# Four sums of the resident weights' quarters move from VectorE to GpSimd

## What is computed

```
h  = layernorm(x)                                # x: 16 x 100 x 1024
q  = h @ Wq                                      # 32 heads of 128
k, v = concat([ctx, h]) @ Wk, ... @ Wv           # ctx: 16 x 361 x 1024; 4 kv heads of 128
x  = x + (softmax(q k^T / sqrt(128)) v) @ Wo
g  = layernorm(x);  inter = g @ c1_w.T @ c2_w.T
idx = argmax of inter in each block of 64 columns (3584 / 64 = 56 rows per token)
x  = x + relu(w1[idx] . g) @ w2t[idx]
```

## Time and profile before

| | us |
|---|---|
| median of 3 runs | 3507.02 |
| the runs | 3506.54 to 3511.08 |
| profiled execution | 3502.41 |
| its span, first to last instruction | 3500.7 |
| TensorE busy (matmul) | 3352.3 (96%) |
| VectorE busy | 2283.3 (65%) |
| ScalarE busy | 1592.1 (45%) |
| GpSimd busy | 1037.2 (30%) |

### The profile page before, as it was taken

One profiled execution on the slowest core, in us unless ns is written; L12 is line 12 of the kernel. 1 busy time (PEld: TensorE's weight loads), 2 busy tenths in 40 slices (PEclk: granted clock), 3 DMA queues, 4 the chain that ended last, 5 costly groups with the idle time before them and its releaser, 6 DMA issues. The chain is left out here.

```text
span 3500.7 us, 52890 instructions
## 1 busy us (share of the span) xinstructions
PE 3352.3 (96%) x18226; PEld 2984.2 (85%) x18226; DVE 2283.3 (65%) x3857; ACT 1592.1 (45%) x3332; POOL 1037.2 (30%) x1220
## 2 busy tenths in 40 slices
PE   6999999799999899999999899999978999999998
PEld 5888888699999899999999778778868999987777
DVE  5555567676766577777777633333337999967776
ACT  4333344344433477777777522232256666621120
POOL 0000000000000377777777210000012455536544
PEclk8999999899999999999999999999999999999999
DMA  3333333355444344333443554454435887889888
GB/s 120 106 100 100 101 97 97 93 129 138 108 129 119 110 114 115 110 111 91 115 115 88 174 134 120 146 155 121 116 125 178 283 306 269 288 311 350 286 286 309
DMA packets 490422, 556.80 MB, mean 159 GB/s; under 512 B 174276, under 2 KB 370372, under 8 KB 490212
## 3 DMA queue, kind: packets, MB, share of 16 engines
q1 hardware_dynamic: 438308, 368.12, 35.4%
q0 software_dynamic: 50848, 183.92, 15.1%
q10 hardware_dynamic: 1056, 2.10, 0.2%
HBM read 440.86 MB, written 113.18 MB: 158 GB/s over the span
## 5 line engine op out<-in xcount | busy, mean ns | idle before, releaser
L2192 PE MATMUL wo_acc<-wo_w,wo_l 128*128 128x512 f32 (+1 forms) x2496 | 577.5, 393 | 20.2 <-DVE wo_l L2142 20.2
L269 PE MATMUL kv_bank<-kv_wo,kv_so 128*128 128x512 f32 x2436 | 574.9, 395 | 16.0 <-DVE kv_wo L361 11.6
L2192 PEld LDWEIGHTS wo_acc<-wo_w,wo_l 128*128 128x128 f32 (+1 forms) x2496 | 462.7, 186 | 134.8 <-DVE wo_w L2166 19.9
L269 PEld LDWEIGHTS kv_bank<-kv_wo,kv_so 128*128 128x128 f32 x2436 | 457.9, 190 | 110.7 <-issue 17.2
L657 PE MATMUL pr_bank<-pr_xo,pr_wp 128*128 128x400 f32 x2688 | 498.4, 347 | 29.0 <-ACT pr_s L724 13.4
L657 PEld LDWEIGHTS pr_bank<-pr_xo,pr_wp 128*128 128x128 f32 x2688 | 493.2, 190 | 31.7 <-DVE pr_wp L741 24.0
L1727 PE MATMUL hid_acc<-x1t,hid_w 128*128 128x304 f32 x2688 | 400.9, 305 | 10.0 <-DVE hid_w L1843 9.9
L2467 PE MATMUL w_acc<-w_w,w_l 128*128 128x512 f32 (+1 forms) x1680 | 385.8, 392 | 9.5 <-DVE w_l L2416 5.2
L1727 PEld LDWEIGHTS hid_acc<-x1t,hid_w 128*128 128x128 f32 x2688 | 382.9, 191 | 12.2 <-DVE hid_w L1843 6.5
L2467 PEld LDWEIGHTS w_acc<-w_w,w_l 128*128 128x128 f32 (+1 forms) x1680 | 307.9, 184 | 87.1 <-DVE w_l L2416 5.2
L2142 DVE TENSOR_TENSOR wo_l<-wo_l_raw,wo_l 128x512 fp32r<-128x512 f32 (+1 forms) x208 | 139.4, 672 | 345.9 <-ACT wo_l L2115 345.8
(11 more groups left out here) (210 smaller groups left out, 4992.1 us busy)
## 6 DMA issues: line engine op xcount, KB each, us to landing
wo_l_raw<-o_scratch SPq DMA_DIRECT2D x192, 256.0 KB, 2.9
pair_raw<-in_L_xattn_Wq_dram SPq DMA_DIRECT2D x64, 512.0 KB, 5.7
q_scratch<-pr_out SPq DMA_DIRECT2D x128, 200.0 KB, 2.4
o_scratch<-o_stage SPq DMA_DIRECT2D x64, 400.0 KB, 3.4
q_raw<-q_scratch SPq DMA_DIRECT2D x64, 384.0 KB, 3.1
stage<-in_ctx_dram SPq DMA_DIRECT2D x45, 512.0 KB, 4.0
h_scratch<-c_raw SPq DMA_DIRECT2D x28, 608.0 KB
wo_w_raw<-in_L_xattn_Wo_dram SPq DMA_DIRECT2D x16, 1024.0 KB, 7.3
```

What stands on the lines that cost most here:

```text
L269: last = pe.matmul(bank[:, BANK[i], :], so[:, i, a, c, :], wo[:, i, e, c, :], start=(not opened and c == 0 and (a, e) == PAIRS[0]), stop=( ...
L2192: last = pe.matmul(acc[p][:rows, :], l[j % 2][:, a, k, :rows], w[:, c, m * per + k, :], start=(m == 0 and k == 0 and (a, c) == PAIRS[0]), ...
```

## The change

GpSimd's program gets the four sums in front of its first copies, with the same waits and the same semaphore; VectorE's loop no longer calls them. Operands, order among the sums and arithmetic stay.

```diff
--- before.py
+++ after.py
@@ -219,7 +219,26 @@
 
         @block.gpsimd
         def _(pool):
+            def sum_b(n):
+                if n == 0:
+                    pool.wait_ge(b_landed[0], 16)
+                    pool.wait_ge(b_landed[1], 16)
+                    last = pool.tensor_tensor(b12, b12, b11, ALU.subtract)
+                elif n == 1:
+                    pool.wait_ge(t_made, 1)
+                    pool.wait_ge(b_low, 2)
+                    last = pool.tensor_tensor(b22, b22, b12, ALU.subtract)
+                elif n == 2:
+                    pool.wait_ge(t_made, 2)
+                    last = pool.tensor_tensor(b11, b22, b11, ALU.subtract)
+                else:
+                    pool.wait_ge(b_low, 4)
+                    last = pool.tensor_tensor(b21, b21, b22, ALU.subtract)
+                last.then_inc(t_made, 1)
+
             pool.memset(moments[:, :], 0.0).then_inc(cleared, 1)
+            for n in range(4):
+                sum_b(n)
 
             for G in range(NG):
                 if pieces(G + 1) > pieces(G):
@@ -413,29 +432,10 @@
                 dve.tensor_tensor(sf[:, 1], pair_raw[G % 2][:, 0, half:, :], sf[:, 1],
                                   ALU.subtract).then_inc(s_made, 1)
 
-            def sum_b(n):
-                if n == 0:
-                    dve.wait_ge(b_landed[0], 16)
-                    dve.wait_ge(b_landed[1], 16)
-                    last = dve.tensor_tensor(b12, b12, b11, ALU.subtract)
-                elif n == 1:
-                    dve.wait_ge(t_made, 1)
-                    dve.wait_ge(b_low, 2)
-                    last = dve.tensor_tensor(b22, b22, b12, ALU.subtract)
-                elif n == 2:
-                    dve.wait_ge(t_made, 2)
-                    last = dve.tensor_tensor(b11, b22, b11, ALU.subtract)
-                else:
-                    dve.wait_ge(b_low, 4)
-                    last = dve.tensor_tensor(b21, b21, b22, ALU.subtract)
-                last.then_inc(t_made, 1)
-
             first_sums(0)
             for k in range(7):
                 low_s(0, k)
                 low_b(k)
-                if k in (0, 1, 2, 3):
-                    sum_b(k)
                 if k == 1:
                     last_sum(0)
             for G in range(NG):
```

## The result

The changed kernel is slower by 0.3%: 3518.08 us median of 7 runs (3516.25 to 3523.79) beside 3508.43 us of the kernel before (7 runs, 3502.27 to 3513.41). The ratio is 1.0031, with a 95% interval of 1.002 to 1.0041, so 7 to 14 us. Its profiled execution took 3519.39 us.

A forecast was written before the change was run, and what follows sets the result against it. The prediction took the start to end with block 4's landing, queued behind a store that waits on VectorE's chain. Exclusion made that chain 8.5 us later; added to the 3507.02 us median this gave 3515.5 us, range 3504.0 to 3520.5.

The forecast's parts named there:

- What bounds the start: First stage: the start ends when context block 4 lands; its load is queued on SyncE behind the first store.
- The 2.92 us: First stage: from the end of VectorE's last low part (46.13) to block 4's issue (49.05), left alone by the change.
- The sum's own length: One 2048-column subtraction on GpSimd: 4.6 us, estimated from rows of 384 and 512 columns.
- Exclusion both ways: GpSimd sums and VectorE's two-SBUF-input instructions shut each other out for whole instructions; chance 0.55.
- The walk: Step-by-step schedule of the start with exclusion, from 16.5 us: last low part ends at 54.7, 8.5 us later.
- First phase: From 16.5 us: GpSimd's first sum and VectorE's low part, small part, low part in turn, 9.6 us, to 26.1.
- Carried one for one: From the start into everything behind it: the 8.5 us delay passes on in full, as no wait has slack.
- the forecast's own: Whole kernel: time range for blocking by whole instructions, 3514 to 3517 us around 3515.5.
- a sign of being wrong: Stages after the first: each keeps its old length; the forecast is wrong if they change by themselves.
- Without exclusion: Rival, start of the first stage: GpSimd doesn't hold VectorE; 2.1 us less, 3504.9, up to 3507; chance 0.15.
- Starved sums: Rival, start: GpSimd gets in only when VectorE runs dry; 13.1 us later, 3520.1; chance of its group 0.17.
- Partial blocking: Rival, start: GpSimd holds the read path for part of a sum; -2 to +7 us, 3505 to 3514; chance 0.13.

The follow-up runs named there:

- kernel with early loads: Kernel before, with loads of context blocks 4 and 5 issued as soon as their buffers are free, ahead of the first store: 3500.03 us beside 3507.17, ratio 0.9977.
- two kernels with early loads: Kernel before and changed kernel, each with blocks 4 and 5 loaded ahead of the first store: 3500.03 us and 3507.22 us.
- the fourth and the first sum alone: Kernel before, with only that one sum on GpSimd, the other three on VectorE; single executions: first 3513.35 us, fourth 3508.84 us.
- write-only kernel: Changed kernel, with each sum replaced by a GpSimd memset of the same tile, same waits and signals: 3506.84 us beside 3508.84, ratio 0.9988.
- with one input: Changed kernel, with each sum replaced by a GpSimd copy of one of its inputs: one execution 3509.44 us, beside 3509.39 of the kernel before.
- with pieces: Changed kernel, with each sum on GpSimd cut into four instructions of 512 columns: 3521.42 us beside 3508.84, ratio 1.0033.

## Why the prediction was right, point by point

- **What bounds the start.** Right, and shown by the kernel with early loads. (A side reading was off: ScalarE is busy for 71 of 200 us in the steady part, a third and not half.) The 2.92 us from the end of the last low part to block 4's issue, which were to stay, are 56.42 - 53.50 = 2.92 us after.
- **The sum's own length.** 4.6 us from the line through two rows; the first one, which waited for nothing, took 4.53.
- **Exclusion both ways.** The chosen reading. The trace of before showed GpSimd standing behind VectorE and hardly the reverse. After it shows VectorE standing for the whole of a sum. The Trainium skill (SBUF — State Buffer, section Who interferes with whom) states it for a VectorE instruction with two SBUF inputs and a GpSimd read, and not against GpSimd work that only writes; both halves agree with runs here (6.59 us beside a sum, 2.29 us beside a memset). The trace of before could have said more than the prediction took from it: the 0.69 us of L1260 beside two-input sums show when VectorE is not shut out.
- **The walk.** First phase to 26.1: VectorE's second low part ended at 25.85. Product 1 at 39.0: 38.09. Fourth sum to 46.9: 45.74. Product 2 at 49.5: 48.31. Last low part to 54.7: 53.50. Block 4 at 57.6: 56.42. Product 3 near 63.4: 61.88. So the order was right, and the sum 1.2 us too long at block 4 and 1.5 at product 3. Part of it is the sum's length (0.07 us each), part is that a low part that was shut out ends 2.15 us after the sum, where the working had 2.2 to 2.3. The rest is spread over single steps, and no run takes it apart.
- **Carried one for one.** The weak term. I held TensorE's restart for equal in both kernels. Its lower clock lasted longer after the gap than in the profiled execution of before, 1.5 us over 36 matmuls, so 7.0 us at product 3 became 8.6 at the end of the stage. But the same 36 matmuls took 9.02 and 9.59 us in the two executions of before, 9.78 to 10.29 in five variants and 10.54 in the changed kernel: before and after happen to be the two ends of eight. How much of the 1.5 us belongs to the change is open. The two kernels with early loads have no such gap, and there the change costs 7.3 us at the end of the stage. So what is shown of the mechanism is 7.0 to 7.3 us; that 8.5 were forecast and 8.6 came is luck, two errors of 1.5 us that cancel.
- **The time.** 3518.08 us lies within the whole range (3504.0 to 3520.5), and 1.1 us above the forecast's own (3514 to 3517). Of the 2.6 us over 3515.5, 1.4 are the kernel before, whose median came out at 3508.43 beside the changed kernel and not at 3507.02. The medians moved by 9.65 us, 1.15 more than forecast.
- **The difference of the two profiled spans** is 17.0 us. 8.6 of it is the first stage. Behind the last product of that stage the program is unchanged, and yet that stretch took 2852.8 us before and 2861.2 after, which the prediction had named as a sign of being wrong. The same stretch took 2855.2 us in the repeated profile of before, 2856.4 and 2860.6 with the fourth and the first sum alone, and 2860.6 to 2862.9 in the write-only kernel, with one input and with pieces. So most kernels with sums moved lie above the two executions of before. But of the two kernels with early loads, the one of before took 2854.9 us and the changed one 2854.2, with the same sums on GpSimd. By the medians the change costs 9.65 us beside 8.6 at the end of the first stage, and 7.2 beside 7.3 with early loads. I take the 8.4 us for scatter of single executions; an effect of 1 us or so on the later stages is not excluded.
- **The rivals.** Without exclusion: forecast 2.1 us faster. The write-only kernel, with 3.5 us for each sum in place of 4.5, came 2.0 us faster by the median, 3.1 by the end of the stage. Starved sums did not come up: each of the four met at most a small VectorE step, waited 0.4 us at the most and then had its turn. Partial blocking is out with the lengths of 6.6 us.

## What to carry to other kernels

An idle engine is not a free one. Before elementwise work goes from VectorE to GpSimd, look whether the VectorE instructions that will run beside it read two SBUF tensors. If so, the moved work stands in VectorE's way for nearly its whole length on GpSimd, here 4.3 us where a low part began just behind a sum, for 2.2 saved. The move can help where VectorE has idle time of that length, where VectorE takes one of its two tensors from PSUM (0.69 us beside a GpSimd subtraction), or where GpSimd only writes. Ahead of that, ask which wait ends last: here one transfer queued behind a store cost 7 us, three times the 2.1 us that the move was worth without exclusion.

## What the runs showed of the hardware

- The time for which VectorE is shut out is inside the reported length of an instruction, not in the idle time in front of it: 6.59 us for a VectorE subtraction of 2048 columns that takes 2.29. VectorE's busy time goes up by it, 7.3 us for four instructions fewer.
- In the run with pieces both engines had work waiting and took turns, one instruction each (pieces of 512 columns: 3.34, 1.74 and 3.34 us on VectorE in turn). That isn't so everywhere: in the kernel before, one indirect transfer on GpSimd took 5.95 us and ended only behind a run of five VectorE instructions.
- A GpSimd copy with one SBUF input shuts out a two-input VectorE instruction too (3.98 us), a memset of 3.51 us does not.
- A VectorE subtraction of an SBUF tensor from one in PSUM isn't shut out by a GpSimd subtraction of two SBUF tensors (0.69 us inside one of 1.29).
- TensorE's return to the higher clock after an idle gap (4.8 to 8.3 us) is not equally quick: the same 36 matmuls took 9.02, 9.59, 9.78, 10.01, 10.11, 10.14, 10.29 and 10.54 us in eight executions.
